# Row 0 of an adjacency product: a third buffer for transposed rows, hand-over by blocks, products of zeros at first, and constants prepared in pieces

## The reference

```python
def L0(x, adj, u, W1, b1, W2, b2, Wg, bg, Wn, bn, g_in, b_in, g_out, b_out):
    x_norm = layernorm(x, g_in, b_in)
    logits = x_norm @ Wn + bn
    y = softmax(logits - log(-log(u)))              # with a hard one_hot forward value
    gate = y[:, 1]
    view2 = (adj * gate[:, None] * gate[None, :]) @ x_norm
    g = sigmoid(concat([x_norm, view2]) @ Wg + bg)
    fused = g * (x_norm @ W1 + b1) + (1 - g) * (view2 @ W2 + b2)
    return layernorm(fused + x, g_out, b_out)

def L1(x, adj, weight, bias):                       # hyperbolic layer
    h = mobius_add(mobius_matvec(weight, x), expmap0(bias))
    support = adj @ logmap0(h)
    return expmap0(relu(logmap0(expmap0(support))))

x = layernorm(x + L0(x, adj, ...))
x = layernorm(x + L1(x, adj, ...))
```

## Time and profile before

| | before |
|---|---|
| median of three executions | 959.79 us (958.04 to 961.1) |
| the profiled execution | 959.55 us, of which 957.8 us are the span of its trace |
| PE busy | 911.9 us, 95% |
| DVE, ACT, POOL busy | 82%, 71%, 24% |
| mean granted TensorE clock | 0.989 |
| moved by transfers | 281.72 MB, mean 294 GB/s |

### The profile page before, as it was taken

One profiled execution on the slowest core, in us unless ns is written; L12 is line 12 of the kernel. 1 busy time (PEld: TensorE's weight loads), 2 busy tenths in 40 slices (PEclk: granted clock), 3 DMA queues, 4 the chain that ended last, 5 costly groups with the idle time before them and its releaser, 6 DMA issues.

```text
span 957.8 us, 12537 instructions
## 1 busy us (share of the span) xinstructions
PE 911.9 (95%) x4032; PEld 720.3 (75%) x4032; DVE 788.0 (82%) x1781; ACT 680.3 (71%) x1214; POOL 232.4 (24%) x201
## 2 busy tenths in 40 slices
PE   4998998999999999999999999998999999999993
PEld 3555776777888878888888888886777878778772
DVE  3658899999989799879686775869899898989886
ACT  4786687878767576757566465666878989789873
POOL 2220212111111121101020010201100764485473
PEclk9999999999999999999999999999999999999997
DMA  7978596876949486958666584566799999999980
GB/s 264 358 282 314 224 424 250 327 316 254 380 192 386 185 350 224 346 190 284 232 253 230 177 304 179 216 258 229 275 355 363 410 375 408 371 402 394 419 333 33
DMA packets 51825, 281.72 MB, mean 294 GB/s; under 512 B 6528, under 2 KB 8496, under 8 KB 20656
## 3 DMA queue, kind: packets, MB, share of 16 engines
q1 hardware_dynamic: 46432, 271.48, 73.8%
q10 hardware_dynamic: 5328, 9.44, 2.8%
HBM read 271.44 MB, written 9.46 MB: 293 GB/s over the span
## 4 chain that ended last, share of the span: by engine, by line
PE 59%; DVE 24%; POOL 5%; ACT 5%; DMA 3%; issue 3%; POOLq 0%; DVEq 0%; SPq 0%; ACTq 0%
PE PS L1023 17%; PE PS L1025 17%; PE PS L1024 17%; DVE AL L761 5%; DVE XGL L761 4%; DVE XTL L761 3%; POOL r_rs L456 2%; PE PS L1112 2%; PE PS L1108 2%; DVE BS L710 2%; PE PS L1021 1%; DMA FU<-in_x_dram 1%; DMA A<-in_adjT_dram 1%; ACT FULL L550 1%; PE PS L1122 1%
## 5 line engine op out<-in xcount | busy, mean ns | idle before, releaser
L565 ACT ACTIVATE AH<-A 128x1024 fp32r<-128x1024 f32 x247 | 252.7, 1057 | 114.1 <-PE PS L1025 92.5
L761 DVE TENSOR_TENSOR AL<-A,AH 128x1024 fp32r<-128x1024 f32 x247 | 294.2, 1218 | 40.6 <-ACT AH L565 39.4
L1023 PE MATMUL PS<-AH,XGH 128*128 128x512 f32 x344 | 139.0, 404 | 4.0 <-DVE AL L761 4.0
L1025 PE MATMUL PS<-AH,XGL 128*128 128x512 f32 x344 | 134.2, 390 | 0.0
L761 DVE TENSOR_TENSOR XGL<-A,XGH 128x1024 fp32r<-128x1024 f32 x113 | 132.2, 1218 | 2.2 <-ACT XGH L565 2.0
L1024 PE MATMUL PS<-AL,XGH 128*128 128x512 f32 x344 | 134.0, 389 | 0.0
L565 ACT ACTIVATE XGH<-A 128x1024 fp32r<-128x1024 f32 x113 | 112.9, 1055 | 13.0 <-DMA A<-in_adjT_dram 11.4
L1023 PE MATMUL PS<-AH,XTH 128*128 128x512 f32 x290 | 114.8, 396 | 3.9 <-DVE AL L761 3.9
L1025 PE MATMUL PS<-AH,XTL 128*128 128x512 f32 x290 | 113.2, 390 | 0.0
L1024 PE MATMUL PS<-AL,XTH 128*128 128x512 f32 x290 | 113.0, 390 | 0.0
L456 POOL TENSOR_TENSOR r_rs<-r_v,NHALF 128x4 f32<-128x4 f32 x24 | 44.4, 1849 | 275.4 <-DVE r_v L716 275.4
(11 more groups left out here) (245 smaller groups left out, 1560.2 us busy)
## 6 DMA issues: line engine op xcount, KB each, us to landing
A<-in_adjT_dram SPq DMA_DIRECT2D x243, 1024.0 KB, 7.1
GB<-gate_scratch SPq DMA_DIRECT2D x12, 256.0 KB, 3.6
XNT<-xnt_scratch SPq DMA_DIRECT2D x12, 256.0 KB, 4.0
XR<-in_x_dram SPq DMA_DIRECT2D x12, 256.0 KB, 4.8
x_scratch<-X SPq DMA_DIRECT2D x12, 256.0 KB, 7.7
xnt_scratch<-XNT ACTq DMA_DIRECT2D x6, 256.0 KB, 4.9
xnt_scratch<-X1T ACTq DMA_DIRECT2D x6, 256.0 KB, 3.9
XR<-in_x_dram ACTq DMA_DIRECT2D x4, 256.0 KB, 6.6
```

The lines of the kernel that those rows point to most:

```text
L565: a.activation(high(m), A[:, n % RING, h * HW:(h + 1) * HW], ACT.Copy).then_inc(S["hi"], 1)
L761: v.tensor_tensor(low(m), A[:, n % RING, h * HW:(h + 1) * HW], high(m).bitcast(F32), ALU.subtract).then_inc(S["lo"], 1)
L1023: p.matmul(acc, hi[:, st], high(m)[:, mv], start=start, stop=False)
L1025: return p.matmul(acc, lo[:, st], high(m)[:, mv], start=False, stop=stop)
```

## The change

Six edits, all in row 0 or at its end:

1. `XNTB` gets a third buffer (HY), so that transposed(k) no longer waits for the store of chunk k-2 but of k-3, and for the logits of k-3.
2. `pre_y` counts single blocks: PE's transposes wait for one normalized block at a time.
3. `xgf` counts single blocks: PE's products of tile (0, q) wait for one gated block at a time.
4. `keep_clock(count)`: PE multiplies `ones` by `BP` (128 x 128 by 128 x 512, bfloat16, zeros at that time) into a bank that no one has used yet; 16 such products before the first transposes and three after each of the first four steps.
5. `prepare` is cut into pieces that run in passes 6 to 10 of DVE's loop, between stats_pre and gate_begin.
6. ACT's copy of `RM` moves behind the splits of halves 24 and 25.

```diff
-        XNTB = (XNT, X1T)
+        XNTB = (XNT, X1T, HY)
...
             def load_x(k):
-                wait_n(act, "pre_y", k - 2)
+                wait_n(act, "pre_y", BLK * (k - 2))
...
-                last.then_inc(S["pre_y"], 1)
+                                 bias=NMP[:, k % 3, t:t + 1], scale=RSP[:, k % 3, t:t + 1]).then_inc(S["pre_y"], 1)
...
-                wait_n(act, "pre_x", k - 1)
-                wait_n(act, f"xnt_stored{k % 2}", 16 * (k // 2))
-                a.activation(XNTB[k % 2][:, :], tbank(k), ACT.Identity, bias=BINC[:, 0:1],
+                wait_n(act, "pre_x", k - 2)
+                wait_n(act, f"xnt_stored{k % 3}", 16 * (k // 3))
+                a.activation(XNTB[k % 3][:, :], tbank(k), ACT.Identity, bias=BINC[:, 0:1],
...
-                last.then_inc(S["xgf"], 1)
+                                 scale=GATE[:, k * BLK + t:k * BLK + t + 1]).then_inc(S["xgf"], 1)
...
-            act.wait_ge(S["rm_psum"], 1)
-            a.activation(RM[:, :], PS[:, 4, 0:P + 1], ACT.Copy).then_inc(S["rm_ready"], 1)
             events, results = first_places(ACT_FIRST), second_places(ACT_SECOND)
             for m in range(2 * NCH, max(2 * NT, last_place(events, results))):
                 if m < 2 * NT:
                     split_high(m)
+                if m == 2 * NCH + 1:
+                    act.wait_ge(S["rm_psum"], 1)
+                    a.activation(RM[:, :], PS[:, 4, 0:P + 1], ACT.Copy).then_inc(S["rm_ready"], 1)
...
-            def prepare():
-                dve.wait_ge(S["weights"], 16 * 6)
-                v.tensor_scalar(RX[:, 0:P], RX[:, 0:P], 0.5, None, ALU.mult)
-                v.tensor_scalar(RS[:, 0:P], RS[:, 0:P], -0.5, None, ALU.mult).then_inc(S["wt_scaled"], 1)
-                dve.wait_ge(S["vecs"], 128)
-                dve.wait_ge(S["const"], 1)
-                link(v.tensor_tensor(B4[:, 0:P], B4[:, 0:P], B4[:, 2 * P:3 * P], ALU.subtract))
-                v.tensor_scalar(B4[:, 0:P], B4[:, 0:P], 0.5, None, ALU.mult)
-                link(v.tensor_scalar(B4[:, 3 * P:], B4[:, 3 * P:], 0.5, None, ALU.mult))
-                for row in (0, 32):
+            def prepare(k):
+
+                if k == 6:
+                    dve.wait_ge(S["weights"], 16 * 6)
+                    v.tensor_scalar(RX[:, 0:P], RX[:, 0:P], 0.5, None, ALU.mult)
+                    v.tensor_scalar(RS[:, 0:P], RS[:, 0:P], -0.5, None, ALU.mult).then_inc(S["wt_scaled"], 1)
+                if k == 7:
+                    dve.wait_ge(S["vecs"], 128)
+                    dve.wait_ge(S["const"], 1)
+                    link(v.tensor_tensor(B4[:, 0:P], B4[:, 0:P], B4[:, 2 * P:3 * P], ALU.subtract))
+                    v.tensor_scalar(B4[:, 0:P], B4[:, 0:P], 0.5, None, ALU.mult)
+                    link(v.tensor_scalar(B4[:, 3 * P:], B4[:, 3 * P:], 0.5, None, ALU.mult))
+                if k in (8, 9):
+                    row = 32 * (k - 8)
                     v.tensor_copy(BP[row:row + 1, :], B4[row:row + 1, :])
                     link(v.tensor_copy(BR[:, :], B4[:, :]))
                     link(v.tensor_tensor(B4[:, :], B4[:, :], BR[:, :], ALU.subtract))
-                v.tensor_copy(BP[64:65, :], B4[64:65, :]).then_inc(S["bias_ready"], 1)
+                if k == 10:
+                    v.tensor_copy(BP[64:65, :], B4[64:65, :]).then_inc(S["bias_ready"], 1)
...
                 if k + 4 < NCH:
                     stats_pre(k + 4)
+                prepare(k)
                 if k + 2 < NCH:
                     gate_begin(k + 2)
                 gated_low(k)
-            prepare()
...
+            def keep_clock(count):
+                for _ in range(count):
+                    p.matmul(PS[:, 1, :], ones[:, :], BP[:, :], start=True, stop=True)
 
             def transposes(k):
-                pe.wait_ge(S["pre_y"], k + 1)
                 wait_n(pe, "pre_xt", k - 1)
                 for t in range(BLK):
+                    pe.wait_ge(S["pre_y"], BLK * k + t + 1)
                     last = p.transpose(tbank(k)[:, blk(t)], YB[k % 2][:, blk(t)], ident)
...
                 for t in (2 * h, 2 * h + 1):
+                    if c == 0 and n < N2:
+                        pe.wait_ge(S["xgf"], BLK * q + t + 1)
...
+            pe.wait_ge(S["const"], 1)
+            keep_clock(16)
+            pe.wait_ge(S["ident_ready"], 2)
             transposes(0)
+            keep_clock(3)
+            pe.wait_ge(S["norm_vecs"], 48)
             rows_and_logits(0)
+            keep_clock(3)
             transposes(1)
+            keep_clock(3)
             rows_and_logits(1)
+            keep_clock(3)
```

More of the change, by code:

```diff
@@ L223, in build @@
                 "gate_arg", "gate_exp", "gates", "xgf", "xgh", "xgl", "gate_tr", "gate_rows", "gate_stored",
-                "xnt_stored0", "xnt_stored1", "epi_in",
+                "xnt_stored0", "xnt_stored1", "xnt_stored2", "epi_in",
                 "hb_sq", "hb_norm", "hb_tanh", "hb_ready", "y2_ready", "rm_psum", "rm_ready", "wt_scaled", "bias_ready",
@@ L396, in _ @@
                     sp.wait_ge(S["gate_stored"], 16)
-                    sp.wait_ge(S["xnt_stored0"], 16 * (NCH // 2))
-                    sp.wait_ge(S["xnt_stored1"], 16 * (NCH // 2))
+                    for i in range(3):
+                        sp.wait_ge(S[f"xnt_stored{i}"], 16 * (NCH // 3))
                     load_front(0)
@@ L514, in store_xnt @@
                 act.wait_ge(S["pre_xt"], k + 1)
-                act.dma_start(xnt_dram[k * P:(k + 1) * P, :], XNTB[k % 2][:, :]).then_inc(S[f"xnt_stored{k % 2}"], 16)
+                act.dma_start(xnt_dram[k * P:(k + 1) * P, :], XNTB[k % 3][:, :]).then_inc(S[f"xnt_stored{k % 3}"], 16)
             for k in range(3):
@@ L527, in normalize @@
                 for t in range(BLK):
-                    last = a.activation(YB[k % 2][:, blk(t)], XIN[k % 3][:, blk(t)], ACT.Identity,
-                                        bias=NMP[:, k % 3, t:t + 1], scale=RSP[:, k % 3, t:t + 1])
-                last.then_inc(S["pre_y"], 1)
+                    a.activation(YB[k % 2][:, blk(t)], XIN[k % 3][:, blk(t)], ACT.Identity,
+                                 bias=NMP[:, k % 3, t:t + 1], scale=RSP[:, k % 3, t:t + 1]).then_inc(S["pre_y"], 1)
             def transposed(k):
@@ L549, in gated @@
                 for t in range(BLK):
-                    last = a.activation(whole(k)[:, blk(t)], xcell(k, t)[:, 0:P], ACT.Copy,
-                                        scale=GATE[:, k * BLK + t:k * BLK + t + 1])
-                last.then_inc(S["xgf"], 1)
+                    a.activation(whole(k)[:, blk(t)], xcell(k, t)[:, 0:P], ACT.Copy,
+                                 scale=GATE[:, k * BLK + t:k * BLK + t + 1]).then_inc(S["xgf"], 1)
             def gated_high(k):
-                act.wait_ge(S["xgf"], k + 1)
+                act.wait_ge(S["xgf"], BLK * (k + 1))
                 a.activation(XGH[:, xcols(k)], whole(k), ACT.Copy).then_inc(S["xgh"], 1)
@@ L728, in neg_mean_pre @@
                 dve.wait_ge(S["pre_rs"], k + 1)
-                wait_n(dve, "pre_y", k - 2)
+                wait_n(dve, "pre_y", BLK * (k - 2))
                 neg_mean(MVP[:, k % 3, :, :], RSP[:, k % 3, :], NMP[:, k % 3, :], "pre_nm")
@@ L1000, in _ @@
             p = nc.tensor
-            pe.wait_ge(S["ident_ready"], 2)
-            pe.wait_ge(S["norm_vecs"], 48)
+            def keep_clock(count):
+                for _ in range(count):
+                    p.matmul(PS[:, 1, :], ones[:, :], BP[:, :], start=True, stop=True)
             def transposes(k):
-                pe.wait_ge(S["pre_y"], k + 1)
                 wait_n(pe, "pre_xt", k - 1)
                 for t in range(BLK):
+                    pe.wait_ge(S["pre_y"], BLK * k + t + 1)
                     last = p.transpose(tbank(k)[:, blk(t)], YB[k % 2][:, blk(t)], ident)
@@ L1012, in rows_and_logits @@
                 pe.wait_ge(S["pre_xt"], k + 1)
-                wait_n(pe, "xgf", k - 1)
+                wait_n(pe, "xgf", BLK * (k - 1))
                 for t in range(BLK):
-                    last = p.matmul(xcell(k, t), XNTB[k % 2][:, blk(t)], IW[:, :], start=True, stop=True)
+                    last = p.matmul(xcell(k, t), XNTB[k % 3][:, blk(t)], IW[:, :], start=True, stop=True)
                 last.then_inc(S["pre_x"], 1)
@@ L1030, in half @@
                 k = n % NCH
-                if c == 0 and n < N2 and h == 0:
-                    pe.wait_ge(S["xgf"], q + 1)
                 if c == 1 and n < N2 and h == 0:
```

## The result

The changed kernel takes 959.66 us in the median of twenty executions, against 958.31 us for the kernel before in as many (twenty, where three were shown above). The ratio is 1.0017, with a 95% interval of [1.0009, 1.0025]; one execution of the changed kernel took 1878.77 us and is left out of it, and without that one the median is 959.48 us. So it is slower by 0.17%. The whole interval lies above 1, though the difference is under the 0.3% that I set as the bound of telling. I had forecast 959.2 us, a gain of half a microsecond (959.55 to 959.0 in the profiled execution, 959.8 to 959.2 in the median of three). The time lies in the range and half a microsecond from the forecast, but the direction is wrong. That it came so close is luck: the three executions that I took as the base have a median 1.5 us over that of the twenty.

What follows compares the result with a forecast made beforehand. The last-ending chain ran 59% over PE and 24% over DVE, with gains counted at `l0`: 2.3 - 1.8 = 0.5 us gained, so 959.55 became 959.0 profiled, 959.2 us median; range 953.5 to 962.0.

Steps and rivals of the forecast that it cites:

- The chain of argument for row 0: Row 0: chunk 4's x load, ending at 26.66 us, sets gated(2) at 30.68; blocks then stay 5.10 us apart.
- my bounds of 0 and 0.8: Start of row 0: the third buffer may bring chunk 4's x load 0 to 0.8 us sooner; 0 was taken.
- my 0.36: End of row 0: a piece of `prepare` delays gate 11, so the gates' store is issued 0.36 us later.
- The failed step: Before `l0`: gates' store done at 81.5 us, three loads again take 6.54, so the gate product runs at 88.0.
- the term of 2.3 us for the start of `l0`: Epilogue's products: they start at 88.75 us rather than 91.08, 2.3 us sooner.
- The clock's price: At `l0`, after PE stands 3.3 us: nine products at the lower clock cost 1.8 us, bounds 0 and 3.6.
- At full clock: Rival at `l0`: it waits but the clock stays up, 2.3 us gained, 957.4 us; chance 0.12.
- The whole stall comes through: Rival before row 1: 3.58 us wait plus 1.8 us slow products gained, 954.3 us; chance 0.28.
- Slower: Rival in DVE's row 0 loop: pieces of `prepare` delay the gates by at most 4.56 us, about 963 us; chance 0.08.
- the ring of row 0: Row 0's cycle between ACT and DVE: gating, normalizing, rounding and DVE's gated_low set 5.10 us per block.
- No effect of the zeros: Rival at row 0's start: the clock falls between the groups of three products anyway, 959.2 us; chance 0.04.
- The sum's small remainder: At `l0`: 2.3 us gained by the earlier start less 1.8 us for the slow clock, 0.5 us gained.

Runs made afterwards that it cites:

- the moved loads: Changed kernel with eight bias vectors' and six weights' loads issued on SP's queue behind the loads of tiles 2 to 5: 959.11 us, ratio 1.0002 to the kernel before.
- its gap filled: Kernel before with 40 bfloat16 products of 128 columns in PE's wait between row 0 and row 1: 957.09 us, ratio 0.9989.
- the early loads: Changed kernel with the epilogue's loads of chunk 0's transposed rows and x issued ahead of tile 15's load: 958.13 us, ratio 0.9994 to the kernel before.

## Why the prediction was wrong

*The chain of argument for row 0 held.* DVE's wait for the x load ended at 26.10 (26.66 before), gated(2) came at 30.13, and the blocks were 5.10 us apart (35.75, 40.85, 45.94). The third buffer removed ACT's wait and changed nothing behind the x load, as said; the load kept its 13.2 us and moved with its issue by 0.55 us, inside my bounds of 0 and 0.8, and less than the 1.61 us by which it differs between two executions of the same code. PE's gap there is 2.37 us and not the 5 I wrote, since PE was with tile (0, 1) until 26.7 us, where I had said 24, and the clock stayed at 1.00 behind it. The zeros were covered by the x load, as said.

*The reason given for it was wrong.* I argued that the load waits behind the store in ACT's queue, and leant on the Trainium skill (DMA: Bandwidth & Descriptors, "Queues, rings and completion order"), which says that a ring's descriptors are consumed in order; it also says that a later one may finish its write before an earlier one, so it didn't carry what I hung on it. With the order turned round the load took 12.8 us all the same. The small loads hold it, as the moved loads show. The windows of the kernel before said it already, had I read them ahead of 26 us: its transfers were almost idle while the load was in flight.

```profile
14.00:16.00 2.00, 1.25 (x6) 1.25 (x7) 1.12 (x8) 1.74 (x5) 0.00 (x0) 1.00 0.20 56
```

*The pieces of* `prepare`: the gates' store would have been issued at 77.28 - 0.55 = 76.73 by the x load; it was at 77.11, 0.38 later, for my 0.36. Counted from the x load's landing in each profile, the store's issue comes after 50.60 to 50.62 us in three kernels without the pieces and 51.04 in the fourth (edits 1 to 4 alone), and after 50.94 to 51.16 in eight with them, so the size is right and the exact match is luck. DVE's first split came at 78.06 (78.65 said), PE's row 1 at 79.43 (79.9), the end of its halves at 85.0 (85.4).

*The failed step is "From 82.40 to 88.94 the three loads took 6.54 us, so the gate product runs at 88.0".* I carried a duration over to another time as if it were fixed. The loads were issued at 81.01, half a microsecond before my 81.5, and took 7.67 us, so the product ran at 88.68; a further 0.2 us went from there to PE. `l0` started at 89.62 and not 88.75, 0.87 us late. So the term of 2.3 us for the start of `l0` was too large: the profile has 1.3 to 1.5 of it, and with the clock held up by products, where the whole 2.3 should have shown, the ratio was 0.9999 with an interval of a tenth of a per cent, so at most about 1 us. The time of the three loads is no constant: where DVE waited for them, from the issue of the first to the product, it was 6.54 us before, 7.67 changed, 7.09 with edits 5 and 6 alone, 7.13 with products ahead of `l0`, 8.09 with the x load before the store, 7.65 without the zeros, 6.57 with the small loads later and 7.32 in the kernel before with its gap filled; with edits 1 to 4 alone it was at most 6.14 (80.61 to 86.75). Two pairs of these have the same code up to that point: 6.54 and 7.32, 7.67 and 7.13. So one profile gave me the time to no better than 0.8 us, and much of my error of 1.1 can be chance. What sets it is open. That the next tiles' loads stand directly behind in SP's queue doesn't order these numbers: they did so at 6.57 and at 7.67, and not at 7.32, where the first of them was issued 1.6 us behind.

*The clock's price was right, its place in the sum was not enough.* Charged 1.8, measured 1.69 in the profiled execution. With the starts it gives the end of `l0`: forecast 0.5 us sooner, measured 0.36 later, and 0.86 is the 0.87 of the failed step. Behind that the last store of x1 was 0.50 us late. The rest of the 1.35 us between the medians is not in this pair of profiles. It may lie in the time at 1.2 GHz, 1.5 to 2.5 us more on average over the executions of the changed kernel, which could cost up to 1.2. Every kernel whose gap was filled lost both (the changed one 3.8 us of it and 1.7 us of time by the ratios; edits 1 to 4, 8.6 and 2.9; before, 5.6 and 1.1). But this isn't shown: without a filled gap the measure doesn't order the kernels (19.7 us with the gates over ACT's queue, 0.19% slower; 21.0 with the early loads, not slower), and over the nineteen executions of the changed kernel it has no correlation with the time (0.0).

*The rivals.* "At full clock" priced `l0` at 2.3 us gained; made true by products, it gave 1.7 us on the changed kernel and no gain on the one before. In that profile `l0` starts 1.6 us sooner than before (89.45 for 91.08), the loads for chunk 1 go out 1.46 us sooner (107.34), and the last store of x1 only 0.86 (672.06), so rows behind `l0` kept some of it. "The whole stall comes through" needed the loads at 85.4; they came at 88.7. "Slower" by the ring of row 0 didn't happen: the pieces moved the gates by some 0.4 us. It was slower though the sum held a gain, because the clock's price came in full and the start of `l0` did not. "No effect of the zeros" came true and was worth nothing, as priced. The sum's small remainder, 2.3 - 1.8, stood on a term known to no better than a microsecond, and gave no ground for a direction.

## What to carry to other kernels

When a wait is taken from in front of an engine, ask what the next wait will be and how long the engine stands there: a stall that is moved, or made longer at one end, can cost more than it did: here TensorE came back from waits of 4.2 us and more at 1.2 GHz, which cost 1.7 us. Where the wait can't be shortened, try filling it with products without use (it gained 0.11% in the kernel before and 0.18% in the changed one), and issue a transfer whose data is ready long before as soon as it is (0.23% less than the changed kernel by itself, 0.47% less with the filled gap). When a load takes several times as long as its neighbours, read the share and the rate of the transfers while it is in flight before blaming its queue: here a low share pointed to the small loads issued beside it, and not to bandwidth. And before a duration or a difference of a microsecond goes into a sum, look how far two executions of the same code lie apart: here it was 0.5 to 0.8 us for one group of loads and 1.6 us for the end of a stage.

## What the runs showed of the hardware

- Fourteen loads of 64 KB or less, issued on SP's queue among the tiles, bring the core's transfers from 424 to 148 GB/s between 12 and 18 us, and a 256 KB load on ACT's queue from 9.1 to 13.2 us. Where they were issued at 20 to 29 us, the rate was 66 GB/s between 28 and 30. Why the transfers stand is not settled here: the rows show that they do, with the share of the 16 DMA engines at 0.27 between 14 and 16 us.
- The load of one row of gates into 128 partitions (256 KB written) took 5.8 to 6.1 us from SP's queue in the three kernels with the other two loads early, and 7.7 us from ACT's in one.
- After a gap of 3.26 us ahead of `l0` the clock stayed at 1.00 in the profiled execution with early loads; gaps of 4.23 to 4.90 us there, in six other kernels, were each followed by 0.50, and the gap of 3.58 us ahead of row 1 in the kernel before by 0.52. The mean over the executions of the kernel with early loads is still 21.0 us at the lower clock, so one profile doesn't tell whether such a gap costs.
- Products of 128 x 128 by 128 columns in bfloat16, 0.056 us from start to start, kept the clock at 1.00 through 2.2 to 2.8 us of filling, followed by waits of 1.35 and 1.49 us.
